# Three tile addresses packed into each word, and the last stage's mixing shared between GpSimd and VectorE, in a graph attention kernel

## What is computed

```python
messages = x[col]
g = (messages @ W_gate.T + b_gate)[:, 0]
h = messages @ W_lin.T + b_lin
e = jnp.exp(g - segment_max(g, row)[row])
attn = e / (segment_sum(e, row) + 1e-16)[row]
pooled = segment_sum(attn[:, None] * h, row)
x = layernorm(x + pooled @ W_out.T + b_out)
```

## Time and profile before

| | |
|---|---|
| median of 3 runs | 3840.32 us (3839.37 to 3845.12) |
| profiled execution, its own time | 3856.86 us |
| its span in the profile | 3855.0 us |
| VectorE busy | 1598.2 us (41%) |
| GpSimd busy | 1645.3 us (43%) |
| TensorE busy, matrix products | 1179.1 us (31%) |
| first gather starts, last add ends | 421.6 us, 3787.9 us |

### The profile page before, as it was taken

The page is one execution under the profiler, slowest core; times in us unless marked ns, Lnnn a source line. Parts: engine busy times, 40 slices in busy tenths (PEclk is TensorE's granted clock), DMA queues, the critical chain, the costliest instruction groups (busy, mean ns, idle before and its releaser), DMA issues.

```text
span 3855.0 us, 26980 instructions
## 1 busy us (share of the span) xinstructions
PE 1179.1 (31%) x5447; PEld 1028.6 (27%) x5447; DVE 1598.2 (41%) x5936; ACT 686.8 (18%) x2101; POOL 1645.3 (43%) x1715
## 2 busy tenths in 40 slices
PE   6221122233322332233322332223322333223352
PEld 4111122222222332222222332223222322222341
DVE  9999422243223432233323432234322432234366
ACT  3110021111211122111211112111211112111214
POOL 1100445434554355544554345544555345543505
PEclk9555555555555655555555555555555555555565
DMA  2000211111111111111111111111111111111122
GB/s 114 41 0 0 63 34 38 37 29 33 38 38 34 29 37 38 38 30 31 39 39 35 29 36 38 38 31 30 38 38 38 29 32 38 38 34 29 37 54 67
DMA packets 88552, 143.50 MB, mean 37 GB/s; under 512 B 28850, under 2 KB 60189, under 8 KB 88271
## 3 DMA queue, kind: packets, MB, share of 16 engines
q0 software_dynamic: 53152, 110.66, 12.9%
q1 hardware_dynamic: 34512, 30.91, 2.4%
q10 hardware_dynamic: 732, 0.20, 0.0%
HBM read 127.84 MB, written 13.83 MB: 37 GB/s over the span
## 4 chain that ended last, share of the span: by engine, by line
another core or an unknown queue 30%; DVE 27%; issue 26%; PE 11%; DVEq 3%; POOL 2%; ACT 1%; DMA 0%; SPq 0%; ACTq 0%; POOLq 0%
DVE nodes_sb L939 11%; PE bank L640 6%; DVE spread L934 3%; PE bank L586 2%; PE bank L620 2%; DVE rows_b L781 2%; POOL ring L405 1%; DVE rows_a L780 1%; DVE rows_a L781 1%; DVE rows_b L780 1%; DVEq L928 1%; DVE turn_b L781 1%; DVE turn_b L780 1%; DVE turn_a L781 1%
## 5 line engine op out<-in xcount | busy, mean ns | idle before, releaser
L405 POOL DMA_INDIRECT ring<-node_table,gather_at x1661 | 1570.8, 946 | 1964.2 <-ACTq L469 1470.5
L640 PE MATMUL bank<-ring,spread 128*128 x3520 | 755.6, 391 | 1866.6 <-DVE nodes_sb L939 1021.3
L934 DVE TENSOR_SCALAR spread<-iota_row,places 128x128 f32<-128x128 f32 x1760 | 498.3, 284 | 1987.5 <-remote 1241.7
L640 PEld LDWEIGHTS bank<-ring,spread 128*128 128x128 f32 x3520 | 674.5, 290 | 1943.5 <-issue 1942.6
L939 DVE SCALAR_TENSOR_TENSOR nodes_sb<-nodes_sb,drops,bank 128x129 f32 x1760 | 612.4, 348 | 3.8 <-issue 1.6
L484 ACT ACTIVATE ring<-ring,weights 128x129 f32<-128x129 f32 x1664 | 545.4, 395 | 359.5 <-issue 359.2
L467 ACT ACTIVATE gather_at<-bank 128x40 int32<-128x40 f32 x42 | 8.5, 203 | 1965.0 <-PE bank L580 1940.2
L620 PE MATMUL bank<-chosen,drop_x 40*128 40x40 f32 x352 | 82.6, 407 | 16.2 <-issue 15.4
L579 PE MATMUL bank<-ident,dst_f 40*128 40x40 f32 x42 | 12.4, 296 | 242.6 <-DVEq L724 228.1
L610 PE MATMUL bank<-chosen,row_f 40*128 40x40 f32 x352 | 83.8, 411 | 6.4 <-DVEq L747 6.4
L586 PE MATMUL bank<-ended,ones 40*128 40x40 f32 x352 | 82.9, 408 | 7.8 <-DVE ended L732 5.6
(11 more groups left out here) (150 smaller groups left out, 1047.7 us busy)
## 6 DMA issues: line engine op xcount, KB each, us to landing
ring<-node_table,gather_at POOLq DMA_INDIRECT x1661
node_table<-ring SPq DMA_DIRECT2D x1, 6347.7 KB
nodes_sb<-in_x SPq DMA_DIRECT2D x10, 625.0 KB
ring<-in_x SPq DMA_DIRECT2D x9, 448.0 KB, 5.3
out<-ring SPq DMA_DIRECT2D x9, 448.0 KB
k<-sorted_keys SPq DMA_DIRECT2D x126, 20.0 KB
rows_a<-in_x SPq DMA_DIRECT2D x2, 448.0 KB
rows_b<-in_x SPq DMA_DIRECT2D x2, 448.0 KB
```

The lines of the kernel that those rows point to most:

```text
L405: pool.indirect_dma_start(out=chunk_rows[c % RING][:, t, :], out_offset=None, in_=table[:, :], in_offset=bass.IndirectOffsetOnAxis(ap=gath ...
L640: last = pe.matmul(tile_ps(slot), lhsT=spread[:, slot, :], rhs=ring[:, bass.ds(got[slot], WIDTH)], start=True, stop=True)
L934: return dve.tensor_scalar(spread[:, slot, :], iota_row[:, :], places[n % 2][:, t:t + 1], None, ALU.is_equal)
```

## The change

Two things are changed together.

First, the numbers of three slots are packed into one word of 24 bits, eight bits each. The tables hold block numbers and tile numbers in place of offsets. Fourteen words hold the forty numbers of a round. Each engine loads them twice a round: six words at batch 0 (slots 0 to 15) and nine at batch 4 (slots 15 to 39). The number of a slot is taken out of its word by a shift and a mask and multiplied by the row's width where it is used.

Second, in the last stage GpSimd works on five of the seven blocks of each group, and VectorE on the other two: one `scalar_tensor_tensor` each that multiplies by the inverse denominator and adds x. VectorE does this for group g+1 ahead of its measuring of group g.

```diff
+PACK, PACK_BITS = 3, 8
+WORDS = -(-T // PACK)
+LOADS = {0: (0, 16), 4: (15, T)}
+POOL_GB = 5
...
+        def unpacked(table, b, engine):
+
+            first, end = LOADS[b]
+            got = nc.values_load_multi_w_load_instructions(
+                table[0:1, first // PACK:-(-end // PACK)], engines=[engine], min_val=0, max_val=(1 << PACK * PACK_BITS) - 1,
+                skip_runtime_bounds_check_because="three numbers of eight bits")[1]
+            return {t: got[t // PACK - first // PACK] >> t % PACK * PACK_BITS & (1 << PACK_BITS) - 1
+                    for t in range(b * BATCH, end)}
...
-                pool.tensor_tensor(mixed[g % Z], here[:, :, 1:WIDTH],
-                                   inv_den[:, g * GB:(g + 1) * GB].unsqueeze(2).to_broadcast([P, GB, FEAT]),
+                into = mixed[g % Z][:, 0:POOL_GB, :]
+                pool.tensor_tensor(into, here[:, 0:POOL_GB, 1:WIDTH],
+                                   inv_den[:, g * GB:g * GB + POOL_GB].unsqueeze(2).to_broadcast([P, POOL_GB, FEAT]),
                                    ALU.mult).then_inc(pooled_ready, 1)
...
-                pool.tensor_tensor(mixed[g % Z], mixed[g % Z], x_at[g], ALU.add).then_inc(resid_ready, 1)
+                pool.tensor_tensor(into, into, x_at[g][:, 0:POOL_GB, :], ALU.add).then_inc(resid_ready, 1)
...
             def normalise(g):
                 act.wait_ge(norm_ready, g + 1)
+                act.wait_ge(rest_mixed, g + 1)
...
             def sum_slots(n):
+                at = {}
...
-                    if b % 2 == 0:
+                    if b in LOADS:
                         pe.nop(nofuse=True)
...
+                        at.update(unpacked(pe_at[n % 2], b, ENGINE.PE))
                     for u in range(BATCH):
                         slot = (b % 2) * BATCH + u
-                        last = pe.matmul(tile_ps(slot), lhsT=spread[:, slot, :], rhs=ring[:, bass.ds(got[slot], WIDTH)],
+                        place = nc.s_assert_within(at[b * BATCH + u], 0, RING * T - 1, skip_runtime_bounds_check_because="a tile's place in the ring")
+                        last = pe.matmul(tile_ps(slot), lhsT=spread[:, slot, :], rhs=ring[:, bass.ds(place * ROW, WIDTH)],
                                          start=True, stop=True)
...
-                dve.scalar_tensor_tensor(dve_at[n % 2][:, :], at[0:1, :], float(-WIDTH), base_cols[:, :], ALU.mult, ALU.add)
+                dve.scalar_tensor_tensor(slot_blocks[:, 0:T], at[0:1, :], -1.0, base_cols[:, :], ALU.mult, ALU.add)
...
-                dve.scalar_tensor_tensor(slot_cols[:, :], wraps[:, :], float(-RING * T), place[:, :], ALU.mult, ALU.add)
+                dve.scalar_tensor_tensor(slot_cols[:, 0:T], wraps[:, :], float(-RING * T), place[:, :], ALU.mult, ALU.add)
                 dve.drain()
-                dve.tensor_scalar(pe_at[n % 2][:, :], slot_cols[:, :], float(ROW), None, ALU.mult)
+                thirds = [v[:, :].rearrange("p (w k) -> p k w", k=PACK) for v in (slot_blocks, slot_cols)]
+                for k in range(2):
+                    dve.scalar_tensor_tensor(packed[:, k, :], thirds[k][:, 2, :], float(1 << PACK_BITS), thirds[k][:, 1, :], ALU.mult, ALU.add)
+                dve.drain()
+                for k, into in enumerate((dve_at, pe_at)):
+                    dve.scalar_tensor_tensor(into[n % 2][:, :], packed[:, k, :], float(1 << PACK_BITS), thirds[k][:, 0, :], ALU.mult, ALU.add)
...
             def slot_values(n, b):
-                many = min(2, batches_of(n) - b) * BATCH
...
+                return unpacked(dve_at[n % 2], b, ENGINE.DVE)
...
             def add_slot(n, t, slot, at_col):
-                here = sums[:, bass.ds(at_col, WIDTH)]
+                here = sums[:, bass.ds(nc.s_assert_within(at_col, 0, BLOCKS - 1, skip_runtime_bounds_check_because="a block's number") * WIDTH, WIDTH)]
...
             def spread_batch(n, b, at, adds=None):
-                if b % 2 == 0:
+                if b in LOADS:
                     dve.nop(nofuse=True)
...
+            def mix_rest(g):
+                if g >= Z:
+                    dve.wait_ge(out_ready, g - Z + 1)
+                dve.wait_ge(x_in[set_of[g]], 16 * (set_of.count(set_of[g]) + (set_of[g] == 2)))
+                for c in range(POOL_GB, GB):
+                    at = (g * GB + c) * WIDTH
+                    dve.scalar_tensor_tensor(mixed[g % Z][:, c, :], sums[:, at + 1:at + WIDTH], inv_den[:, g * GB + c:g * GB + c + 1],
+                                             x_at[g][:, c, :], ALU.mult, ALU.add)
+                dve.drain().then_inc(rest_mixed, 1)
...
+            mix_rest(0)
             for g in range(GROUPS):
+                if g + 1 < GROUPS:
+                    mix_rest(g + 1)
                 dve.wait_ge(resid_ready, g + 1)
```

More of the change, by code:

```diff
@@ L87, in check_shapes @@
     assert BLOCKS % GB == 0 and GROUPS % 2 == 0
+    assert max(RING * T, BLOCKS) <= 1 << PACK_BITS and PACK * PACK_BITS <= 24 and SLOTS > (ROUNDS - 1) * T + T - BATCH
 def tiles_of(c):
@@ L183, in graph_attention @@
         slot_rows = [sb(f"slot_rows{k}", [P, T]) for k in range(2)]
-        slot_cols = sb("slot_cols", [1, T])
+        slot_cols, slot_blocks = sb("slot_cols", [1, PACK * WORDS]), sb("slot_blocks", [1, PACK * WORDS])
+        packed = sb("packed", [1, 2, WORDS])
         window_at = sb("window_at", [T, WINDOW, WINDOW])
@@ L190, in graph_attention @@
         place, wraps = sb("place", [1, T]), sb("wraps", [1, T])
-        dve_at = [sb(f"dve_at{k}", [1, T], I32) for k in range(2)]
-        pe_at = [sb(f"pe_at{k}", [1, T], I32) for k in range(2)]
+        dve_at = [sb(f"dve_at{k}", [1, WORDS], I32) for k in range(2)]
+        pe_at = [sb(f"pe_at{k}", [1, WORDS], I32) for k in range(2)]
         pen = [sb(f"pen{k}", [T, 2, P]) for k in range(2)]
@@ L679, in _ @@
             dve.tensor_scalar(base_rows[:, :], iota_row[:, 0:T], float((WINDOW - 1) * T), float(P), ALU.add, ALU.mult)
-            dve.tensor_scalar(base_cols[:, :], iota_row[0:1, 0:T], float((WINDOW - 1) * T), float(WIDTH), ALU.add, ALU.mult)
+            dve.tensor_scalar(base_cols[:, :], iota_row[0:1, 0:T], float((WINDOW - 1) * T), None, ALU.add)
+            dve.memset(slot_cols[:, :], 0.0)
+            dve.memset(slot_blocks[:, :], 0.0)
             for k in range(LOG_ROWS):
@@ L926, in slot_values @@
             def slot_values(n, b):
-                many = min(2, batches_of(n) - b) * BATCH
-                got = nc.values_load_multi_w_load_instructions(
-                    dve_at[n % 2][0:1, b * BATCH:b * BATCH + many], engines=[mybir.EngineType.DVE],
-                    min_val=0, max_val=(BLOCKS - 1) * WIDTH, skip_runtime_bounds_check_because="a block times the width")[1]
-                return {b * BATCH + k: got[k] for k in range(many)}
+                return unpacked(dve_at[n % 2], b, ENGINE.DVE)
             def spread_slot(n, t, slot):
```

5 lines of the change are left out of this document (1 added, 4 removed).

## The result

The changed kernel takes 4220.93 us (median of 4 runs, 4216.57 to 4224.21), the kernel before 3839.85 in the same comparison: 1.099 times as long, 95% interval 1.097 to 1.101. The prediction had 3877 (1.009) and a range to 3960. The direction was right, the size was not: +381 us where +36 was forecast. The profiled execution spans 4222.4 us.

A forecast was written before the change was run, and what follows sets the result against it. The prediction took VectorE's chain of dependent adds after the gathers as the bound. Loads -11, address steps +42 and last stage +5 gave +36 us, 3877 us against a median of 3840.3; the range ran from 3822 to 3960.

The forecast's parts named there:

- VectorE's address steps: Between two adds on VectorE: shift, mask and multiplication add 0.03 us in each of 1410 slots, +42 us.
- TensorE's address steps: TensorE's records after the gathers stand beside longer matrix work; only a batch's first counts, taken at 0.
- loads: Fewer address loads gain 0.24 us before batch 8 in 44 rounds, -11 us; bounds 0 and 79 us.
- last stage: At the end, VectorE takes two of seven blocks: +5 us, between -6 without port collisions and +21 with them.
- the second wait: VectorE's wait before batch 3, 18.94 us, follows the gathers' end: 4.98 or 5.70 us after the last, still about 5.
- the price of a slot: Added VectorE time per slot between two adds: 0.03 us, one longer instruction, with bounds of 0 and 0.18.
- two instructions more per slot: Rival: shift and mask not joined with product and sum on VectorE, 0.18 us a slot, 254 us, 4088 us; chance 0.13.
- The load of nine words: Address load at batch 4: one load of 0.67 us if time goes by words, 0.07 more.
- two loads of 0.60: Rival: nine words need two loads, VectorE then TensorE lose 0.6 us each, 53 us more, 3930 us; chance 0.12.
- the upper bound of 79: Most that dropped loads before batches 2, 6 and 8 could gain if all exposed: 3 x 0.60 x 44 us.
- `place_slots` and the memsets at 0: Some 0.6 us of extra packing lies before a 26.86 us wait, the memsets beside input loads: 0; uncovered packing, 26 us.

The follow-up runs named there:

- early loads: Kernel before, nothing packed, both engines loading 8 words before batch 0 and the other 32 before batch 2: 3783.63 us against 3850.29, ratio 0.983.
- aligned loads: Changed kernel with the last stage of before and two loads of 8 words, from words 0 and 8, before batches 0 and 6: 4072.85 us, ratio 1.059.
- multiplication alone: Kernel before with tables of block and tile numbers, multiplied where used, no shift or mask: 3871.80 us against 3855.98, ratio 1.0035.
- VectorE's addresses packed, aligned: Kernel before with only VectorE's addresses packed, in two loads of 8 words: 4042.50 us against 3855.98, ratio 1.047.
- both packed: Changed kernel with the last stage of before: 4211.02 us, ratio 1.095.
- both packed, wait on the add: Changed kernel with the last stage of before and the wait for the previous add moved onto the add itself: 4018.88 us, ratio 1.045.

## Why the prediction was wrong

The direction and the main place were right: the path is VectorE's chain after the gathers, and what stands between two adds counts in every slot. A load ahead of the waits inside the gathers costs nothing, not even one of 32 words (early loads). But the second of these waits, which the prediction took as fixed, grew. Each of the four terms was too small, and by the runs they were worth:

| term | forecast | measured |
|---|---|---|
| VectorE's address steps | +42 | +187 (with aligned loads, its fewer loads in it) |
| TensorE's address steps | 0 | +30 to +44 |
| loads | -11 | +138 against aligned loads |
| last stage | +5 | +11.5 |
| sum | +36 | +367 to +381 (measured whole: +381) |

The traces split a round into three stretches. The gathers take 49.7 or 49.8 us in all of these kernels; the other two, in us, as means of 39 rounds, with the mean granted clock of the last stretch (a mean of both levels):

| kernel | last gather's end to batch 3 (the second wait) | batch 3 to the next first gather | clock there |
|---|---|---|---|
| before | 5.22 | 24.28 | 0.66 |
| multiplication alone | 5.24 | 24.71 | 0.62 |
| VectorE's addresses packed, aligned | 5.51 | 28.25 | 0.58 |
| both packed, aligned | 6.27 | 28.25 | 0.56 |
| both packed | 6.22 | 31.38 | 0.56 |
| both packed, wait on the add | 6.13 | 27.07 | 0.65 |
| changed kernel | 6.09 | 31.49 | 0.55 |
| early loads, nothing packed | 4.96 | 22.83 | 0.71 |

- **The step that failed first is the price of a slot**, "I take 0.03". The traces give +0.131, and 1410 x 0.131 is 185 us. The argument for it, that one record does all that a slot needs and so would go on doing it, holds for the multiplication alone (+0.011, 15 us). Shift and mask are instructions of their own. The rival *two instructions more per slot* had the mechanism and said 0.18 and 4088 us; it took two for every slot, and a third of them have one, with 0.08 us for each instead of 0.086. Its 254 us stand against the 217 to 231 of the first two terms. It was given 0.13, and the range left it out. The 187 need not all be in the steps themselves: in the stretch from batch 3 on, where most of it lies (24.28 to 28.25 us), the clock falls from 0.66 to 0.58 and a record of TensorE's products grows from 0.377 to 0.419 us. What the clock alone costs was not separated.
- **TensorE's steps at 0** failed too, and not where the prediction had looked. It said that only the first of a batch counts, and then dropped that one. In the traces the stretch from batch 3 on is as long with TensorE's addresses packed as without (28.25 us both), but the second wait is 0.76 us longer, 32 us in 42 rounds. So the loss lies there and not in a price for each batch.
- **The load of nine words** was bounded by 0.67 and, as a rival, by two loads of 0.60. It took 2.07, since neither the number of words nor the number of loads was what mattered but the word it starts at. The place was right: that rival said that VectorE and then TensorE would pay before VectorE's batch 6, as they do.
- **Loads worth 11 us.** Before batch 8 the idle time went, as forecast. But with the loads before batches 4, 6 and 8 gone on both engines the kernel gains 67 us (early loads), near the upper bound of 79 that the prediction set aside; the clock of the stretch is higher there too (0.71 for 0.66). What the changed kernel saves of this with its two loads isn't separated from the rest.
- **The second wait** was to end about 5 us after the last gather. In the round shown it ends 6.33 us after (2110.32 against 2103.99). Its length comes in steps of about 0.7 us (4.3, 5.0, 5.7, 6.4), so means tell more than single rounds: 6.09 against 5.22 before, worth some 37 us in 42 rounds. It grows when TensorE's addresses are packed too (5.51 to 6.27), hardly with VectorE's alone and not with the multiplication (5.24), and moving the wait to the add does not bring it back (6.13). So these 37 us are in the first two terms of the table, not beside them. How the shifts and masks reach this wait the trace does not show; that cause stays open.
- **The last stage** came out inside its bounds. VectorE's measuring of a group starts 3.13 to 5.62 us after that of the group before, with a mean of 4.55 against 3.89 before (the prediction's 3.4 to 5.3). The new operations collide with GpSimd as it was described; the shift step, which the prediction let pay its 0.66 further on, nearly ceases to (0.17 in thirteen of fourteen groups). The Trainium skill, page "SBUF — State Buffer", section "SBUF: two separate sides", has VectorE's instruction with two SBUF inputs wait for the whole of a GpSimd instruction that reads SBUF and started first; the 2.38 us for two operations beside GpSimd against 0.61 without it agree.
- **`place_slots` and the memsets at 0**: nothing in the runs speaks against it, since the aligned kernel has them too and its loss is accounted for, but no run took them out.

## What to carry to other kernels

Arithmetic on a register that becomes an address is paid where the wait stands. If the engine first waits and then works the address out, every ALU step lies on the chain of dependent operations; put the wait on the operation itself, and the same steps run while the one before is under way (-192 us here). Measure it where it will run: on the second kind of chip the same move made the kernel before 0.3% slower. Before trading loads for arithmetic, ask what a load costs by its start and not only by its length, and whether it can simply be issued earlier, in front of a wait that is there anyway: that gained 67 us here with nothing packed. And check a wait taken as fixed against the trace after: the one that the prediction had end at 5 us moved by 0.9 us a round. Last, see on which chip the time was taken: an edit worth 5% on one was worth 0.6% on another, because there a different engine ended last.

## What the runs showed of the hardware that was not expected

- A register load of VectorE costs about 0.09 us and 0.25 for each four words when it starts at word 0 or 4, and about 0.23 for every single word when it starts at word 5 (2.07 us for nine; the loads from words 1, 2, 7 and 8 are among those not used). The Trainium skill, page "DMA: Bandwidth & Descriptors", section "Latency and other measured facts", gives a floor of some 600 ns for such a load; here 4 words took 0.357, so for this kernel the measurement decides. Its page "Runtime: NRT & Kernel Launch", section "Instruction fetch mechanics", has about 200 ns for each register even in bulk, for the loads from HBM that the runtime puts in. The loads here come from SBUF: those from word 5 are near that price (0.23), the aligned ones far below it (1.107 us for 16 words).
- A queue joins a multiplication into its address step (+11 ns on VectorE, +9 on TensorE) but not a shift or a mask (45 and 36 ns each, 0.08 us from add to add).
- Chips differ by 1.44 times in the time of the same kernel (3856 and 2675 us). On the one kind VectorE, and ScalarE some 16 us into a burst of gathers, nearly stand still until the burst is over; on the other they do not, and the gathers follow each other from round to round. The trace does not name what they wait for ("issue", "remote"), and no experiment was made on it: this is the largest item in the kernel's time, and it stays open.
